# A third buffer of one-hot rows in the edge aggregation of a graph and mixture-of-experts layer

## What is computed

```python
h = feats * rsqrt(deg_out)[:, None]
m = segment_sum(h[src], dst, num_segments=n) * rsqrt(deg_in)[:, None]
x = m @ W_gc + b_gc + (feats @ W_res + b_res)
y = x + moe_ff(x)        # top 2 of 64 experts, 256 -> 512 -> 256, gelu
# y is normalised over the nodes, feats is added, and each row is normalised
```

## Time and profile before

| What | us |
|---|---|
| median of 3 runs | 2977.45 |
| the runs | 2967.4, 2977.49, 2977.45 |
| profiled execution, device time | 2967.47 |
| its span, first to last instruction | 2965.7 |
| TensorE busy | 2067.3 |
| VectorE busy | 1235.3 |
| GpSimd busy | 1885.7 |

### The profile page before, as it was taken

One profiled execution on the slowest core, in us unless ns is written; L12 is line 12 of the kernel. 1 busy time (PEld: TensorE's weight loads), 2 busy tenths in 40 slices (PEclk: granted clock), 3 DMA queues, 4 the chain that ended last, 5 costly groups with the idle time before them and its releaser, 6 DMA issues.

```text
span 2965.7 us, 44135 instructions
## 1 busy us (share of the span) xinstructions
PE 2067.3 (70%) x10204; PEld 1712.2 (58%) x10251; DVE 1235.3 (42%) x3115; ACT 410.3 (14%) x1358; POOL 1885.7 (64%) x1969
## 2 busy tenths in 40 slices
PE   8956556566665666666767776777758898999670
PEld 7944444454444545555555565656647788888650
DVE  8971212223223333444445445555562222222267
ACT  3010000000000001010111111111112222232213
POOL 0017777777777777777777777777725677777500
PEclk6557777777878888888989989999978899999885
DMA  8033333333333333333333333333324456666532
GB/s 295 0 102 107 106 106 106 106 107 108 108 107 108 110 107 110 110 109 109 111 110 111 109 112 111 111 111 113 111 70 121 140 182 198 196 192 186 169 124 87
DMA packets 205082, 362.76 MB, mean 122 GB/s; under 512 B 43080, under 2 KB 125814, under 8 KB 204814
## 3 DMA queue, kind: packets, MB, share of 16 engines
q0 software_dynamic: 93648, 230.69, 26.9%
q1 hardware_dynamic: 104058, 123.31, 13.1%
q10 hardware_dynamic: 7108, 6.43, 0.6%
HBM read 327.91 MB, written 57.52 MB: 130 GB/s over the span
## 4 chain that ended last, share of the span: by engine, by line
POOL 33%; PE 28%; issue 18%; DVE 8%; DMA 6%; DVEq 4%; ACT 1%; PEld 1%; POOLq 1%; ACTq 1%; SPq 0%; PEldq 0%
POOL ring L456 16%; POOL stage L456 16%; PE bank L1264 7%; PE bank L1148 7%; PE bank L1258 5%; DMA ring<-nodes,slots 3%; PE bank L1128 3%; PE bank L1189 2%; PE bank L1249 1%; PE bank L1168 1%; DMA stage<-y 1%; DVE stage L744 1%; DMA ring<-table,ring_idx 1%; DVE slots L844 1%; DVE acc L1046 1%
## 5 line engine op out<-in xcount | busy, mean ns | idle before, releaser
L456 POOL DMA_INDIRECT ring<-table,ring_idx x792 | 749.3, 946 | 241.9 <-issue 240.4
L456 POOL DMA_INDIRECT stage<-table,ring_idx x771 | 729.1, 946 | 234.7 <-issue 231.5
L1148 PE MATMUL bank<-ring,hot 128*128 128x257 f32 x1056 | 305.2, 452 | 163.1 <-DMA ring<-table,ring_idx 153.9
L1148 PE MATMUL bank<-stage 128*128 128x257 f32 x1030 | 304.1, 459 | 135.4 <-DMA stage<-table,ring_idx 126.0
L1148 PEld LDWEIGHTS bank<-ring,hot 128*128 128x128 f32 x1056 | 237.3, 231 | 224.9 <-issue 142.1
L1148 PEld LDWEIGHTS bank<-stage 128*128 128x128 f32 x1030 | 236.3, 235 | 197.5 <-issue 101.1
L940 DVE TENSOR_TENSOR acc<-acc,bank 128x257 f32 x196 | 82.9, 423 | 560.7 <-PE bank L1148 523.9
L480 POOL DMA_INDIRECT ring<-nodes,slots x192 | 200.7, 1045 | 93.0 <-issue 58.9
L490 POOL DMA_INDIRECT y<-ring,slots x192 | 198.3, 1033 | 90.3 <-issue 55.6
L1258 PEld LDWEIGHTS bank<-ring,stage 128*128 128x128 f32 x1984 | 239.0, 198 | 11.7 <-issue 6.6
L1258 PE MATMUL bank<-ring,stage 128*128 128x128 f32 x1984 | 241.5, 281 | 4.1 <-issue 1.7
(11 more groups left out here) (226 smaller groups left out, 2478.1 us busy)
## 6 DMA issues: line engine op xcount, KB each, us to landing
stage<-in_L_gnn_w_dram SPq DMA_DIRECT2D x128, 512.0 KB
ring<-table,ring_idx POOLq DMA_INDIRECT x792
y<-zeros SPq DMA_DIRECT2D x49, 256.0 KB, 2.1
stage<-y SPq DMA_DIRECT2D x14, 896.0 KB, 7.1
stage<-table,ring_idx POOLq DMA_INDIRECT x771
stage<-in_L_gnn_b_dram SPq DMA_DIRECT2D x64, 128.0 KB
nodes<-yS ACTq DMA_DIRECT2D x49, 128.0 KB
xs<-in_x_dram SPq DMA_DIRECT2D x1, 6144.0 KB
```

The lines of the kernel that those rows point to most:

```text
L456: pool.indirect_dma_start(out=ring(q)[:, j, 0:D], out_offset=None, in_=table[:, :], in_offset=bass.IndirectOffsetOnAxis(ap=ring_idx[:, q, ...
L1148: last = pe.matmul(bank[:, 0:D + 1], hots[:, j, :], ring(q)[:, j, :], start=j == 0, stop=j == n - 1)
```

## The change

`HOTS` goes from 2 to 3, with a new tensor `hot_mid` for the third buffer (and a third row of `dstq`). Before the first step VectorE makes the rows of two groups in place of one. In the iteration of group g it makes the rows of group g+2 in place of g+1. The wait is for the matmuls of group g-1 in both versions, since the buffer that is written was used by the group three back in place of two back. TensorE picks the buffer by `hot[q % HOTS]`, and its code is otherwise the same.

```diff
-HOTS = 2
+HOTS = 3
...
         hot_low = sb("hot", [P, CPG, P])
-        hot = (hot_low[:, :, :], stage[:, high0:high0 + CPG * P].rearrange("p (j d) -> p j d", j=CPG))
+        hot_mid = sb("hot_mid", [P, CPG, P])
+        hot = (hot_low[:, :, :], stage[:, high0:high0 + CPG * P].rearrange("p (j d) -> p j d", j=CPG), hot_mid[:, :, :])
...
-            one_hots(0, 0, True)
+            for g in range(HOTS - 1):
+                one_hots(0, g, True)
...
-                    if q + 1 < (LASTQ if final else RING):
-                        one_hots(it, q + 1, first)
+                    ahead = q + HOTS - 1
+                    if ahead < (LASTQ if final else RING):
+                        one_hots(it, ahead, first)
                     elif not final:
-                        one_hots(it + 1, 0)
+                        one_hots(it + 1, ahead - RING)
```

## The result

The changed kernel is slower: a median of 2983.62 us (2976.47 to 2994.61, 18 runs) against 2971.7 us for the kernel before (2965.4 to 2979.66, 18 runs). The ratio is 1.0036, with a 95% interval of 1.0024 to 1.0048, so 7 to 14 us lost and some 11 us at the middle. I had forecast a gain of 1.5 us. The loss is within the 0.5% that I had called no change, but it is clear of scatter and of the wrong sign.

A forecast was written before the change was run, and what follows sets the result against it. Gathers bound the edge stage until 1753 us, then TensorE, VectorE and ticks. Between a 4.2 us gain and a 1.4 us loss it took about 1.5 us gained: 2977.45 - 1.5 = 2976 us, range 2961 to 2984 us.

The forecast's parts named there:

- The bound, and what costs nothing: First 1541 us of the edge stage: gathers set the pace, so 31.6 us of TensorE's one-hot waits cost nothing.
- the tail: Edge stage from 1753 us to its end: TensorE, VectorE and ticks bound it; gain there at most 18.4 us.
- The waits: In the tail, 25.1 us of own-row waits go; extra-row waits grow from 25.1 us to 40 or more.
- the clock's: Slow matmul sets behind moved loop-top gaps at 170, 181 and 187: 5.6 us lost if it happens each time.
- the 4.2 us of the sum: Gains at loop tops, a three-group period and the stage's end: 1.7 + 1.1 + 1.0 + 0.4 us.
- The clock gets worse: Rival: moved gaps cost full price and some ticks behind run slow, 2980 to 2985 us; chance 0.18.
- The larger gain: Rival: extra rows come earlier too and the tail catches up with the gathers, 2959 us; chance 0.08.
- nothing moved: Rival: something other than one-hot rows came last before the matmuls, so the time stays 2977 us; chance 0.08.
- a stall that grows: Rival: a second VectorE stall of the loop-top sort in the loop body, 19 us over six steps, 2997 us; chance 0.06.
- the two readings: Absence of long gaps keeps the full clock: fewer waits gain 4.2 us, or moved gaps lose 1.4 us.
- The base: Time of the whole kernel before, from which the forecast counted: 2977.45 us, the median of three runs.

The follow-up runs named there:

- two_of_three_b: The changed kernel with HOTS back at 2, the third buffer there but unused; ratio 0.9991 to the kernel before.
- waits_back_b: The changed kernel with TensorE also waiting for the next group's one-hot rows ahead of a group's matmuls; ratio 0.9994 to the kernel before.
- load_early3_b: The changed kernel with the first extra tile's rows made first and the next group's code loaded behind the rows made; ratio 0.9967 to the kernel before.
- waits_top_b: The changed kernel with TensorE's wait for the next group's rows put back only at each step's second group; ratio 1.0012 to the kernel before.
- waits_short_b: The changed kernel with that wait put back at every group but each step's second; ratio 1.0036 to the kernel before.
- filler_b: The changed kernel with six short unused matmuls ahead of TensorE's wait for an extra tile's rows; ratio 1.0011 to the kernel before.

## Why the prediction was wrong

**The bound, and what costs nothing** were right. From 200 to 1741 us TensorE still waits mostly for the gathers after the change, and the 31.6 us of waits for one-hot rows there were worth nothing. Two signs of the tail failed: group 195 was to start 14 to 20 us after its gathers allow it, and starts 38.0 us after (2208.91 less 2167.94 + 2.99); the gathers were to end near 2164 us and ended at 2167.94. In two_of_three_b and waits_back_b, whose TensorE waits as before, the lags are 24 and 25 us.

**The waits** went where the prediction said: 25.1 us to 2.8 for own rows, 25.1 to 46.5 for the extra rows, of which it had asked 40 or more. That the extra rows end the periods is borne out by load_early3_b, where making them earlier shortened the tail until the gathers were late again.

**The term that failed is the clock's.** The prediction bounded it at 5.6 us and took half of that. It measured 23.1 us in the trace after. By the ratio, which is that of 18 runs, the net loss is 11 us; if the gain was the 4.2 us of the sum, the usual cost of the clock is some 15 us, by my estimate. Its one priced part, slow sets behind the loop tops, came out near its bound: 5.4 us more in the extra matmuls there. What it left out is the rest, in three steps. First, the tick behind such a set was given no price, and ticks right behind loop tops cost 7.1 us more. Second, sets and ticks away from the loop tops were put at nothing, though I had the slow ticks of the kernel before in the same view (4 of 19); they cost 10.6 us more. Third, I took the gap as moved but unchanged. At the top of the step of 186 TensorE had been idle 3.8 us, then ran 5.4 us of matmuls, then waited 0.2. Without the first wait, and with these matmuls done at the full clock ahead of the gap, one wait of 6 us is left. The gap behind which I had seen 5.83 us for a set was 5.74 us long, and after the change five of the six loop tops have one of 5.95 us or more.

**The rivals.** "The clock gets worse" was the right mechanism, with a chance of 0.18, and priced at 3 to 8 us over now; it came to 12 between the medians of 18 runs. What I had put against it, that the gaps are no longer than before, was false at five of six loop tops. The larger gain and nothing moved did not happen. Nor did a stall that grows: VectorE's idle time for issuing ahead of `dstq` in the tail is 31.5 us in 26 places in both kernels. Against "nothing moves" I had given 0.05 us between rows and matmuls; the sum shown there gives 0.12 us, since it leaves out the 0.07 us between VectorE's two instructions. Nothing hangs on it.

**The Trainium skill's rule** ("TensorE: Matmul & The Clock Gate", the section "Why this matters for your kernels") had the two readings that the prediction gave. The second was the right one, and the 1.4 us that I had made of it falls short of the 11. Fewer waits did not mean shorter gaps.

**The base** was too high as well. I worked from the median of three runs, 2977.45; the median of 18 is 2971.7. That the measured 2983.62 us lies among the 2980 to 2985 us of the right rival, and at the upper edge of the range as a whole, is luck: from 2971.7 us the same prices would have ended at 2980 us.

**What stays open.** That the removed waits cause the loss is shown (waits_back_b), and that most of it hangs on the long ones is made likely (waits_top_b against waits_short_b). That the time is lost by way of the clock rests on filler_b, where work was only added, and on the clock cost, which goes with the lag from trace to trace. Why ticks away from the loop tops ran slow more often after the change, and how many of them do in a usual execution, I could not settle.

## What to carry to other kernels

Before removing a wait from TensorE, look for the next wait behind it that stays. If another engine ends the period anyway, the waits join into a longer one. Here such an idle stretch was charged twice: in itself, and in the lower clock of the work behind it, which then stood on the path. Bring forward what ends the period first (here the extra tile's rows, with the load that they need hidden beside other work), and ask of every instruction moved which load or register read moves with it.

## What the runs showed that I had not expected

The gathers seem to have two paces. Two kernels of one batch, whose gathers are the same, ended them 4.6 us apart. The last gather in two_of_three_b and in waits_back_b:

```profile
2168.43 0.95 POOL L457 DMA_INDIRECT stage<-table,ring_idx  x1 [0.30 <-issue]
```

```profile
2163.84 0.95 POOL L457 DMA_INDIRECT stage<-table,ring_idx  x1 [0.30 <-issue]
```

In the ten traces at the usual time, six have it at 2163.3 to 2163.9 us and four at 2167.9 to 2168.6. That is 0.2% on each of 1563 gathers. Both ends of it occur with two buffers and with three, so it looks like scatter between executions, of 4 to 5 us, and not like a kernel's doing; one trace of each kernel can't show more. What sets the pace no run shows. A trace of one kernel at one pace and of another at the other differ by this much, so the lag, counted from the last gather, compares them better than the span.

An added wait that made a kernel faster, and added matmuls that did, were the other surprise: 0.9994 against 1.0036, and 1.0011 against 1.0036.
